# TensorE's first-attention loop over 16 tiles instead of twice 8, with node updates in mid-step

## What is computed

```python
# layer 0, "typed": keys are shifted by a vector of the edge's relation
Q = ((x + 0.1*query) @ Wq + bq);  K, V = the same with Wk, Wv        # 4 heads x 64
scores = einsum(Q[dst], K[src] + 0.2*rel_w[type]) / 8
w = softmax of scores over the edges of one dst;  agg = segment_sum(w * V[src], dst)
x1 = layernorm(x + layernorm_affine(agg @ Wo + bo + x))
# layer 1, "plain": xp = x1 @ W; alpha = leaky_relu(a_src[src] + a_dst[dst])
out = layernorm(x1 + elu(segment_sum(softmax(alpha) * xp[src], dst) + bias))
```

## Time and profile before

| what | us |
|---|---|
| timed runs, median of 3 | 4472.4 |
| profiled execution, span from first to last instruction | 6181.0 |
| first attention, first to last gather | 350.7 to 3278.6 |
| second attention, first to last gather | 3359.6 to 6124.0 |

### The profile page before, as it was taken

How to read it: one execution, slowest core, us unless ns; L and a number is a source line. 1 busy time by engine, 2 the same in 40 slices (tenths; PEclk the granted TensorE clock), 3 DMA queues, 4 the chain that set the end, 5 groups by cost and what they waited for, 6 DMA issues and landing times. The chain is left out here.

```text
span 6181.0 us, 164556 instructions
## 1 busy us (share of the span) xinstructions
PE 4261.5 (69%) x50798; PEld 2746.6 (44%) x50798; DVE 3295.8 (53%) x10527; ACT 2576.2 (42%) x6781; POOL 3049.7 (49%) x3229
## 2 busy tenths in 40 slices
PE   7958878777778787778786555555555555555554
PEld 4634444444444444444443444444444443444443
DVE  3235555555555555555554455555555555555555
ACT  2323344444444444444343444444444444444444
POOL 1245555545555555555452555555555555555553
PEclk9989999999999999999997666656566566565666
DMA  7856676666666666666664555555555555555554
GB/s 224 282 163 191 185 189 186 186 186 185 186 187 183 186 186 187 185 186 186 184 185 114 145 153 156 152 151 153 152 153 153 150 152 149 154 152 152 154 150 123
DMA packets 820553, 1055.91 MB, mean 171 GB/s; under 512 B 458633, under 2 KB 632338, under 8 KB 820464
## 3 DMA queue, kind: packets, MB, share of 16 engines
q0 software_dynamic: 225072, 730.03, 42.9%
q1 hardware_dynamic: 594078, 324.02, 20.6%
q10 hardware_dynamic: 1314, 0.99, 0.1%
HBM read 919.46 MB, written 133.59 MB: 170 GB/s over the span
## 5 line engine op out<-in xcount | busy, mean ns | idle before, releaser
L766 POOL DMA_INDIRECT typed_rows<-kv,typed_index x1563 | 1491.3, 954 | 1470.8 <-remote 570.5
L1298 POOL DMA_INDIRECT plain_rows<-xp,plain_index x1563 | 1486.0, 951 | 1359.5 <-remote 536.1
L875 PE MATMUL typed_p_s<-typed_kt,typed_q 64*32 64x416 f32 x4168 | 835.7, 549 | 336.6 <-issue 289.7
L997 DVE CUSTOM_DVE_ANT_0 typed_weight<-typed_p_s,typed_far 128x416 f32<-128x416 f32 x521 | 308.3, 592 | 1113.6 <-PE typed_p_s L875 1080.8
L1400 PE MATMUL plain_p_o<-plain_rows,plain_weight_t 128*32 128x65 f32 x16672 | 630.5, 296 | 331.5 <-issue 310.7
L1433 DVE SCALAR_TENSOR_TENSOR plain_p_s<-plain_p_s,plain_a_dst,plain_damped 128x416 f32<-128x416 f32 x521 | 342.3, 657 | 865.9 <-ACT plain_damped L1553 475.1
L1389 PE MATMUL plain_p_s<-all_cst,plain_rows 128*128 128x128 f32 x2084 | 546.2, 395 | 346.0 <-issue 319.6
L1375 PE MATMUL plain_p_w<-all_cst,plain_weight 128*128 128x128 f32 x1563 | 437.5, 404 | 431.6 <-issue 286.0
L1400 PEld LDWEIGHTS plain_p_o<-plain_rows,plain_weight_t 128*32 128x32 f32 x16672 | 459.2, 154 | 556.6 <-issue 516.7
L1167 ACT ACTIVATE typed_weight<-typed_weight,typed_col 128x416 f32<-128x416 f32 x521 | 334.7, 642 | 806.6 <-issue 549.7
L1389 PEld LDWEIGHTS plain_p_s<-all_cst,plain_rows 128*128 128x128 f32 x2084 | 406.0, 210 | 463.6 <-issue 437.6
(11 more groups left out here) (191 smaller groups left out, 6936.5 us busy)
## 6 DMA issues: line engine op xcount, KB each, us to landing
typed_match<-match SPq DMA_DIRECT2D x131, 208.0 KB
plain_match<-match SPq DMA_DIRECT2D x131, 208.0 KB
agg<-qkv_zero SPq DMA_DIRECT2D x98, 264.0 KB
typed_agg<-agg SPq DMA_DIRECT2D x98, 264.0 KB
plain_agg<-agg SPq DMA_DIRECT2D x98, 264.0 KB
kv<-qkv_kv SPq DMA_DIRECT2D x98, 258.0 KB
typed_kinds<-match SPq DMA_DIRECT2D x131, 192.0 KB
typed_rows<-kv,typed_index POOLq DMA_INDIRECT x1563
```

Source lines behind the costliest of these rows:

```text
L766: pool.indirect_dma_start(rows[:, r, j, :], None, k.kv, bass.IndirectOffsetOnAxis(ap=index[:, g, at:at + 1], axis=0)).then_inc(rows_in[r], 16)
L875: last = pe.matmul(p_s[at:at + TN, 0:SLOTS], q[own, m, :, h // 2], kt[own, h // 2, lo:lo + SLOTS], start=True, stop=True, tile_position=(H ...
L1298: pool.indirect_dma_start(rows[:, r, j, :], None, k.xp, bass.IndirectOffsetOnAxis(ap=index[:, g, at:at + 1], axis=0)).then_inc(rows_in[r], 16)
```

## The change

The loop of TensorE over two times eight steps becomes one loop over 16 steps, written out; 25 steps stand ahead of it instead of nine, so it makes 31 passes. `update` and `move` no longer stand ahead of a step but inside it, after `score` and before `relate`. The wait for `copy_message` moves with them, to the `aggregate` of the next step; the third block's `move` stands two steps after its `update`, as the others' do. The wait of `update` for `put` now names the tile summed in the same step. On ScalarE `copy_message` stands behind `copy_weights` and `put` of its step instead of ahead of them.

```diff
-    PE_FIRST = 9
+    PE_FIRST, BLOCK0 = 25, 13
...
-                        pe.wait_ge(result_ready, TILES if static else n - LAG)
+                        pe.wait_ge(result_ready, results)
...
-            def step(t, copied=None):
-                for part in (TilePart(TURN_LAG, turn_weights), TilePart(LAG, lambda b: aggregate(b, copied)), TilePart(SCORE, score),
-                             TilePart(0, relate), TilePart(KEY, arrive)):
-                    part.at(t)
+            def step(t, copied=None, middle=None):
+                TilePart(TURN_LAG, turn_weights).at(t)
+                TilePart(LAG, lambda b: aggregate(b, copied)).at(t)
+                TilePart(SCORE, score).at(t)
+                if middle is not None:
+                    middle()
+                TilePart(0, relate).at(t)
+                TilePart(KEY, arrive).at(t)
...
+            def nodes(t, v, place):
+                if place == 0:
+                    return None, lambda: update(v, t.n - LAG + 1)
+                if place == 1:
+                    return v + 2, None
+                if place == 2:
+                    return None, lambda: move(v)
+                return None, None
+            def block_step(t):
+                at = t.c - BLOCK0
+                for shift in (0, 2 * GAP, 3 * GAP):
+                    if t.c >= BLOCK0 and 0 <= (at - shift) % PERIOD <= 2 and at >= shift:
+                        v = t.q * GROUP + (at - shift) // PERIOD * GROUP + (0, 2 * GAP, 3 * GAP).index(shift)
+                        return nodes(t, v, (at - shift) % PERIOD)
+                return None, None
...
-                with pe.Fori(0, 2) as half:
-                    for c in range(PE_FIRST, PE_FIRST + HALF):
-                        copied = None
-                        if c == PE_FIRST:
-                            copied = q_ * GROUP + half + 1
-                        if c == PE_FIRST + GAP:
-                            update(q_ * GROUP + half, q_ * PERIOD + half * HALF + c)
-                            copied = q_ * GROUP + half + 2
-                        if c == PE_FIRST + GAP + 2:
-                            move(q_ * GROUP + half)
-                        step(Step(q_ * 2 + half, c, HALF), copied)
-                update(q_ * GROUP + 2, q_ * PERIOD + PERIOD + PE_FIRST)
-                move(q_ * GROUP + 2)
+                for c in range(PE_FIRST, PE_FIRST + PERIOD):
+                    step(Step(q_, c, PERIOD), *block_step(Step(q_, c, PERIOD)))
...
-            interleave(act, FIRST, BlockPart(2, 1, copy_message), TilePart(TURN_LAG + 1, copy_weights), TilePart(LAG + 1, put), TilePart(SCORE + 1, weigh), TilePart(1, copy_relations), TilePart(SCORE, set_apart),
+            interleave(act, FIRST, TilePart(TURN_LAG + 1, copy_weights), TilePart(LAG + 1, put), BlockPart(2, 1, copy_message), TilePart(SCORE + 1, weigh), TilePart(1, copy_relations), TilePart(SCORE, set_apart),
```

More of the change, by code:

```diff
@@ L891, in aggregate, with update @@
                 last.then_inc(agg_done, 1)
-            def update(v, n, static=False):
-                within = lambda lag: not static or v - lag < ROWS
+            def update(v, results):
+                within = lambda lag: not isinstance(v, int) or v - lag < ROWS
                 pe.wait_ge(x1_t_ready, v + 1)
@@ L929, in _ @@
             for n in range(PE_FIRST):
-                step(Step(0, n, HALF))
+                step(Step(0, n, PERIOD), *block_step(Step(0, n, PERIOD)))
             with pe.Fori(0, (TILES - PE_FIRST) // PERIOD) as q_:
-                with pe.Fori(0, 2) as half:
-                    for c in range(PE_FIRST, PE_FIRST + HALF):
-                        copied = None
-                        if c == PE_FIRST:
-                            copied = q_ * GROUP + half + 1
-                        if c == PE_FIRST + GAP:
-                            update(q_ * GROUP + half, q_ * PERIOD + half * HALF + c)
-                            copied = q_ * GROUP + half + 2
-                        if c == PE_FIRST + GAP + 2:
-                            move(q_ * GROUP + half)
-                        step(Step(q_ * 2 + half, c, HALF), copied)
@@ L943, in _ @@
-                update(q_ * GROUP + 2, q_ * PERIOD + PERIOD + PE_FIRST)
-                move(q_ * GROUP + 2)
-            v = (TILES - PE_FIRST) // PERIOD * GROUP
-            for n in range(TILES, TILES + LAG):
[L947 to L955, removed]
+                for c in range(PE_FIRST, PE_FIRST + PERIOD):
+                    step(Step(q_, c, PERIOD), *block_step(Step(q_, c, PERIOD)))
@@ L956, in _ @@
+            for n in range(TILES, TILES + LAG):
+                step(Step(0, n, PERIOD), *block_step(Step(0, n, PERIOD)))
+            v = (TILES - PE_FIRST) // PERIOD * GROUP + GROUP
+            move(v)
+            for v in range(v + 1, ROWS + PROJECT):
+                update(v, TILES)
                 move(v)
-                v += 1
         @block.vector
```

## The result

The changed kernel takes 4731.38 us, the median of five runs (4721.02 to 4737.60), against 4472.87 us for five runs of the kernel before beside it: a ratio of 1.057 (95% interval 1.0557 to 1.0583), some 258 us slower.

The account below looks back on a forecast made before the run. GpSimd's gathers were taken to bound timed runs, at a floor of 4416 us. The message wait's 75 us of profiled span became 54 of a run, other terms 0; 30 were credited: 4472.4 - 30 = 4442 us, range 4400 to 4510.

Parts of the forecast that it names:

- The size of the loop: TensorE's doubled loop body, about 1885 instructions: taken at 0 a pass, at most 3.9 us, 121 us over 31 passes.
- The loop no longer stays resident: Rival: TensorE waits for instructions at each of 31 passes, up to 3.9 us; 4505 to 4539 us; chance 0.27.
- the ring of eight slots: Gather ring of eight tiles: could absorb a 3 us stall if TensorE is otherwise faster than the gathers.
- The wait for the message: TensorE's sums waiting for ScalarE's message copy: falls from 1.50 to 0.51 us, saving 75 us of the profiled span.
- What the update now delays: VectorE's keys come 1.4 us later at three steps of 16: cost nothing, bounds some 20 us either way.
- DMA is near its limit too: First attention: 3.88 us of all 16 engines per tile, no less than GpSimd's 3.75; faster TensorE does not move it.
- GpSimd's floor: Back-to-back gathers, 1953.8 us per attention, plus starts, ends and first waits: a run needs at least 4416 us.
- The room: Timed median above GpSimd's gather minimum: 56 to 197 us; a little over half, 30 us, given to the first attention.
- The old branch: TensorE's inner loop branch shows no idle time, hidden by queued matmuls, so writing the loop out saves 0.
- Hidden anyway: Rival: gathers or DMA already pace the first attention, so TensorE's stall is made up; 4472 us; chance 0.33.

Follow-up runs that it names:

- e2_small_loop: The changed kernel with TensorE's loop again two inner passes of eight steps, third block's update and move together behind the inner loop: 4495.44 us, ratio 1.006.
- e3_written_out_only: The kernel before, old order, with only the two inner passes written out as 16 steps: 4629.26 us, ratio 1.0361.
- e4_no_spill_sums: The changed kernel without the sums over each tile's 32 spilled edges, a written-out body of 1629 instructions: 4468.81 us, ratio 1.000.
- second profile of before: The kernel before, unchanged, profiled again: span 4468.3 us in a run of 4472.16 us.
- e7_split_update: The kernel before, small loop kept; for two blocks of three only update's transposes move to mid-step, behind the scores: 4444.61 us, ratio 0.9944.
- padded kernel with 107 instructions: The changed kernel with 118 spare transposes ahead of the written-out steps, so the loop begins 107 instructions before its first piece's end: 4668.22 us, ratio 1.0446.

## Why the prediction was wrong, point by point

The forecast was 4442 us and the range ended at 4510; the time is 4731.

**The step that failed is "The size of the loop".** It took 0 a pass, because the nearest row was the old loop's, 16 pieces in all. But that row shows a body of half the size; it bounds the price from below and says nothing at twice the size. In its place the runs show 8.2 us a pass. The mechanism was the rival "The loop no longer stays resident", at 0.27. The count of about 1885 instructions was right, and so was the sign to look for: hundreds of pieces, and idling without a releaser ahead of the turning of weights once per pass. `e2_small_loop` (17 pieces), `e3_written_out_only` (299) and `e4_no_spill_sums` (25) show the cause: the body's size, with either order. The body of 1629 instructions over 7 pieces is kept, that of 1885 over 8 or 9 is not.

The Trainium skill ("Runtime: NRT & Kernel Launch", Instruction fetch mechanics), which the prediction weighed against that row, gives TensorE 2048 instructions in blocks of 256, so 8 blocks, and says that a taken branch whose target is not in "the current 2-page window" waits for a DMA. The runs agree on a wait at the branch, 3.6 us in the mean. They do not agree with a window of two blocks, since the loop of 1629 instructions over 7 pieces is kept; nor do all 8 blocks serve, since a loop that touches eight pieces is already fetched anew. Where between 1629 and 1885 instructions the limit lies, and whether it goes by instructions or by pieces touched, no run shows. The prediction took the 2048 from this section and left out the window of two, with which the old loop, kept at about half of 1885 instructions, does not agree either.

**The rival's price was mis-sized as well.** "No longer stays resident" was to cost at most 3.9 us a pass, the longest wait of the earlier trace rows, so 121 us. It costs 13.53 - 5.31 = 8.2 us a pass. The first of the 31 passes is entered without the branch, and its step takes 5.26 us; 30 branches back are 247 us, against 251 lost in the first attention. The stall at the branch alone, 106.5 / 30 = 3.6 us, is near the 3.9, but by luck: that row is a wait of the second attention (L1375). Two terms were missed. There is a second stall at the first piece's end, 75.2 / 30 = 2.5 us, so 6.1 us together. And the matmuls behind them run at a granted clock of 0.5. Of the windows above, 2.03 + 1.93 us of busy time at 0.50 to 0.53 would take half at 1.00, and 2.30 us at 0.74 would take 1.7: some 2.5 us lost, about the 2.1 that remain. The cover that the rival allowed, the ring of eight slots, is not there: GpSimd's waits for slots between 1000 and 2000 us went from

```profile
POOL typed_rows L766 <- PE typed_p_o L889: 48.0, 66, 1.4
```

in the second profile of before to

```profile
POOL typed_rows L766 <- PE typed_p_o L889: 163.8, 98, 7.7
```

after. The loop already needed more per tile (3.90 us) than the gathers (3.75), so it could not make a stall up.

**The wait for the message: right in kind, too large.** It vanishes as foreseen, but the 90.2 us of the earlier trace rows are those of the one long execution; in the second profile they are 23.1 us, in 31 cases of 98 blocks, where the prediction took 53 cases for too few. Taking 75 us from that row and scaling it by the ratio of spans left 54 us of a run, over twice what there was.

**"What the update now delays" is not free.** It was costed at nothing between bounds of 20 us either way. After, the 15 steps away from place 8 sum to 57.2 us, before to 57.1, though after's hold one move more; over all 16, `e4_no_spill_sums` and before both take 62.4: the order is neutral. The sums no longer wait, but the keys come later by the whole update, and the step with an update at place 4 takes 4.70 us instead of 4.45, that with a move at place 6 takes 4.68 instead of 3.95; the steps behind them are shorter. What the message gave, the scores took back, by their wait for VectorE's keys: in the second profile of before the two waits are 23.1 + 198.9 = 222.0 us, in `e2_small_loop` the scores alone wait for 226.3. `e7_split_update` delays the keys by the transposes alone, waits for 186.5 us and is 25 us faster than before. It differs from `e2_small_loop` in where the loop begins and in the third block too, so the split was not tried by itself.

**"DMA is near its limit too"** came from the long execution as well. There a tile took 3.88 us of all 16 engines; in the second profile of before it takes 0.91 x 2024 / 521 = 3.54 us, less than the gathers' 3.75 (estimates from the shares).

**What held.** GpSimd's floor: the second attention sits 10 us above it in every profile compared here. The room lies between the 56 and 197 us of the prediction, at 69 + 10 = 79, but it is almost all the first attention's, where "a little over half" was assumed. The old branch cost nothing to begin with: in neither the second profile of before nor `e4_no_spill_sums` does TensorE wait without a releaser at L860. No kept loop of the old order was written out, so that writing out saves nothing by itself is not shown beyond this. "Hidden anyway" would have been the result of the order alone, but for another reason than its own: not because GpSimd paces the first attention, but because one wait of TensorE, for ScalarE's copy, is exchanged for another, for VectorE's keys.

What stays open: why the first profiled execution of before took 1.38 times as long as a run.

## To carry to other kernels

Before a loop is written out, count its instructions on the engine that has the most, in pieces of 16 KB from where it begins, and treat a body that passes the largest one seen to be kept as a cost per pass, not as free; that a smaller loop is kept says nothing about a larger one. Where the instruction queue's line grows from some 20 pieces to hundreds, the price is read from the first steps behind the branch, second stall and lower clock included, and it moves with the loop's place in memory. Before waits are priced from a profile, compare its span with the timed runs, and take a second profile where they differ. When a piece of work is moved past a wait, move only what the wait needs, and look at which engine waits for what is now delayed: the four transposes helped, the whole update in front of the keys did not.

## What the runs showed of the hardware beyond this

- A pass's price depends on where the loop begins: one body of 1885 instructions took 4564, 4668 or 4731 us with 243, 107 or 87 instructions left in its first piece.
- Behind the first two pieces the fetches cost nothing visible: nine to ten come per branch back ((315 - 25) / 30 = 9.7), TensorE has two stalls, and its other 15 steps take 57.2 us, as against 57.1 where nothing is fetched anew.
- After an idle time of 2.6 us TensorE's granted clock was 0.5 for some 7 us; in the padded kernel with 107 instructions its scores still ran in 0.90 us behind a first stall of 2.54 us.
